# Graph attention with layer norm: the turned source one-hots of two chunks are stored interleaved, element beside element

## The reference, cut to what matters

```python
q = (X @ Wq)[src]; k = (X @ Wk)[dst]
e = tanh(q + k)                               # E x 64
scores = e @ Wphi; scores -= max(scores)
w = exp(scores)
denom = segment_sum(w, src, N)
alpha = w / (denom[src] + 1e-9)
msg = alpha[:, None] * ((X @ Wy_w + Wy_b)[dst] + e @ We)
out = layernorm(X + segment_sum(msg, src, N))
```

## Time and profile before

| | us |
|---|---|
| median of 3 runs | 5431.57 (5428.85 to 5432.63) |
| profiled execution, its own time | 5425.74 |
| span of the profiled execution | 5424.0 |
| busy: PE / DVE / ACT / POOL | 3511.2 / 4216.0 / 3684.6 / 3537.4 |
| indirect gathers of line 1112 | 3276, from 1161.8 to 5309.8 |
| one-hot makers of line 1182 | 206, from 1187.1 to 5291.0 |

### The profile page before, as it was taken

The page is one execution under the profiler, slowest core; times in us unless marked ns, Lnnn a source line. Parts: engine busy times, 40 slices in busy tenths (PEclk is TensorE's granted clock), DMA queues, the critical chain, the costliest instruction groups (busy, mean ns, idle before and its releaser), DMA issues. The chain is left out here.

```text
span 5424.0 us, 91419 instructions
## 1 busy us (share of the span) xinstructions
PE 3511.2 (65%) x19333; PEld 2746.3 (51%) x19333; DVE 4216.0 (78%) x9852; ACT 3684.6 (68%) x14197; POOL 3537.4 (65%) x3559
## 2 busy tenths in 40 slices
PE   7799999955555665555655555556655555556557
PEld 7566566644444444444444444444544444444446
DVE  7699999977777777777777777777777777777776
ACT  3699999966666666666666666666666666666667
POOL 1034434357777777777777777777777777777771
PEclk9899999977777767777777777776677777777778
DMA  3200000023333333333333333333333333333334
GB/s 89 73 5 5 5 5 5 5 71 106 106 106 102 106 106 107 103 106 106 106 103 107 106 105 103 106 107 105 104 106 107 106 103 106 106 105 102 106 98 110
DMA packets 284190, 478.09 MB, mean 88 GB/s; under 512 B 94226, under 2 KB 203892, under 8 KB 283385
## 3 DMA queue, kind: packets, MB, share of 16 engines
q0 software_dynamic: 165184, 324.30, 23.0%
q1 hardware_dynamic: 100662, 142.95, 7.8%
q10 hardware_dynamic: 17794, 4.91, 0.4%
HBM read 456.43 MB, written 20.60 MB: 88 GB/s over the span
## 5 line engine op out<-in xcount | busy, mean ns | idle before, releaser
L1112 POOL DMA_INDIRECT gathered<-table,dst_rows x3276 | 3151.2, 962 | 1008.9 <-issue 992.1
L1146 PE MATMUL bank<-gathered,weighted_onehots 128*128 128x193 f32 x6592 | 1913.4, 455 | 1458.6 <-DVE block_sums L1235 1450.4
L1146 PEld LDWEIGHTS bank<-gathered,weighted_onehots 128*128 128x128 f32 x6592 | 1582.1, 267 | 1661.9 <-issue 997.4
L1235 DVE TENSOR_TENSOR block_sums<-block_sums,bank 128x193 f32 x3296 | 1166.8, 354 | 541.1 <-issue 166.0
L1198 DVE TENSOR_REDUCE gathered<-bank 128x128 f32<-128x384 f32 x1648 | 840.5, 552 | 446.0 <-DMA gathered<-table,dst_rows 435.0
L1157 ACT ACTIVATE gathered<-gathered 128x256 f32<-128x256 f32 x824 | 346.5, 421 | 1202.8 <-DVE gathered L1202 1202.8
L1167 ACT ACTIVATE weighted_onehots<-src_distances,score_less_shift 128x128 f32<-128x128 bf16 x3296 | 1052.4, 390 | 26.9
L1175 ACT ACTIVATE src_distances<-row_to,src_in_block 128x128 bf16<-128x128 f32 x3296 | 1039.6, 386 | 0.0
L822 ACT ACTIVATE places_past_far<-bank,stat 128x98 bf16<-128x98 f32 x2727 | 889.2, 1237 | 18.8 <-PE bank L847 18.8
L822 ACT ACTIVATION_READ_ACCUMULATOR places_past_far<-bank,stat 128x1 f32 x2727 | 887.9, 1097 | 0.0
L1135 PE MATMUL bank<-q_parts,src_onehots_T 128*128 x3296 | 614.7, 317 | 272.6 <-DVE gathered L1202 231.2
(11 more groups left out here) (190 smaller groups left out, 2272.5 us busy)
## 6 DMA issues: line engine op xcount, KB each, us to landing
src_in_block_rows<-src_in_block_list SPq DMA_DIRECT2D x206, 512.0 KB
gathered<-table,dst_rows POOLq DMA_INDIRECT x3276
gathered<-table SPq DMA_DIRECT2D x2560, 0.8 KB
table<-in_x SPq DMA_DIRECT2D x4, 1562.5 KB
x_in<-in_x SPq DMA_DIRECT2D x24, 256.0 KB, 2.9
x_again<-in_x SPq DMA_DIRECT2D x48, 128.0 KB, 2.3
out<-out_rows SPq DMA_DIRECT2D x48, 128.0 KB, 1.9
sorted_list<-sorted_groups,unit_destinations POOLq DMA_INDIRECT x248
```

Source lines behind the costliest of these rows:

```text
L1112: e.indirect_dma_start(slot[:, r, j, 0:ROW], None, table, bass.IndirectOffsetOnAxis(ap=gidx[:, t:t + 1].bitcast(u32), axis=0)).then_inc(ga ...
L1146: made = e.matmul(SM[q % 2 * 2 + j // 2][:, o:o + SUMS], ohw[:, q % 3, j, :], slot[:, r, j, A:SLOT], start=True, stop=True)
L1235: e.tensor_tensor(sums[:, bass.ds(b, SUMS)], sums[:, bass.ds(b, SUMS)], SM[q % 2 * 2 + j // 2][:, o:o + SUMS], ALU.add).then_inc(accumulat ...
```

## The change

The buffer `ohT` keeps its size, but its last two dimensions are swapped. Before, the 2048 bf16 columns of one chunk lay behind the 2048 of the other. Now column `i` of the even chunk lies at place `2 i` and column `i` of the odd chunk at `2 i + 1`. VectorE's compare of line 1182 therefore still reads `lob` element after element, but writes every second bf16 element, and the weight loads in front of the matmuls of line 1135 read every second one. No instruction, wait or transfer is added, removed or moved: the order of the instructions of every engine is the same.

```diff
-        ohT = sb(lists, "src_onehots_T", [PARTS, 2, CHUNK * PARTS], bf16)
+        ohT = sb(lists, "src_onehots_T", [PARTS, CHUNK * PARTS, 2], bf16)
...
-                        made = e.matmul(QK[q % 2][j // 2][:, j % 2 * 3 * A:(j % 2 + 1) * 3 * A], ohT[:, c % 2, o:o + PARTS], q3[:, bass.ds(b, 3 * A)],
+                        made = e.matmul(QK[q % 2][j // 2][:, j % 2 * 3 * A:(j % 2 + 1) * 3 * A], ohT[:, o:o + PARTS, c % 2], q3[:, bass.ds(b, 3 * A)],
                                         start=True, stop=True)
...
-            e.tensor_scalar(ohT[:, c % 2, :], lob[:, c % LOB, :], part0[:, :], None, ALU.is_equal).then_inc(onehots_T_made, 1)
+            e.tensor_scalar(ohT[:, :, c % 2], lob[:, c % LOB, :], part0[:, :], None, ALU.is_equal).then_inc(onehots_T_made, 1)
```

## The result

The changed kernel takes 5556.75 us (median of four, 5554.93 to 5558.66), the kernel before 5430.73 us. The ratio is 1.0228, with a 95% interval from 1.0212 to 1.0243: 126 us slower, where 109 (5540 against 5431.6) were forecast.

What follows compares the result with a forecast made beforehand. The prediction took GpSimd's gathers, held up by VectorE's compare, as the bound. It added 108 us to the profiled 5425.7, giving 5534, or 5540 as a median, 2.0% slower, with a range of 5500 to 5575 us.

Steps and rivals of the forecast that it cites:

- The gathers are the bound and have no slack: GpSimd's gathers, line 1112, run through the main part without a stop, 4148 us from first to last start.
- The compare drops to two elements at a time: Line 1182, writing every second element, falls to 0.517 ns an element from 0.261.
- The rival of the plain rate: Line 1182 falls to one element at a time, 2.33 us, and no longer holds gathers; 5407 us, chance 0.10.
- The length of the compare, 1274 ns: Line 1182: 2048 x 0.517 + 215 = 1274 ns, 0.52 us more than now.
- the hold: While line 1182 runs, VectorE locks GpSimd out of a shared port pair, delaying gathers; 25 us in all before the change.
- the dense middle rate: VectorE's two elements at a time, 0.517 ns an element, taken from four-byte operands in lines 584 and 287.
- The near row, line 589: Nearest profile row with a strided 2-byte output: 242 ns for 124 elements, against 229 at 0.517 ns an element.
- Each hold moves the gather's end by as much as it grows: At line 1112, a compare longer by 0.52 us puts each following gather 0.52 us later; 206 x 0.52 = 108 us.
- The phases stay: Compares keep their places against the gathers; other phases would give 89 to 142 us.
- VectorE's own path costs nothing: 107 us more VectorE busy time, 0.52 of 5.1 us idle in a chunk, is hidden; without cover up to 107 us.
- TensorE's reads cost nothing: Line 1135's weight loads, reading every second element, taken as nothing; at most 0.65 us in a step.

Runs made afterwards that it cites:

- the f32 and strided-source probes: The changed kernel with twelve forms of the compare, six times each, run at its end while other engines are idle; 6183.82 us on another chip.
- the summing form: The compare also sums its output into an unused number, in the changed kernel and in the kernel before; ratios 0.9985 and 1.0010 on another chip.
- the reduction: The kernel before, with an unused VectorE reduction of 1024 numbers added behind each of the 206 compares; 5421.22 us, ratio 0.9987.
- the read-only kernel: The kernel before with its dense compare, but query matmuls read a small fixed buffer of zeros with a step of two; 5426.84 us, ratio 1.0000.
- the kernel with two compares: The kernel before, with the dense compare made twice in a row, the second behind a wait for the first; 5462.36 us, ratio 1.0065.
- write_only: The changed kernel with its strided compare, but query matmuls read a small fixed buffer of zeros without a step; 5557.64 us, ratio 1.0228.
- the kernel with halves: The kernel before, with its dense compare split into two halves, one in this step and one in the next; ratios 1.0012 and 1.0011 on two other chips.

## Why the prediction was right, point by point

- *The gathers are the bound and have no slack.* Right. 128 us more in the gathers are the 126 of the median, and 249 us of other VectorE work changed nothing. It held for the chip of the prediction; on the two others GpSimd also waited for what the profile calls remote, and for TensorE.
- *The compare drops to two elements at a time.* Right, by the f32 and strided-source probes, which take the same time. The rival of the plain rate is out for this compare: it would have taken 2.3 us. Its second half, that a compare at the plain rate does not hold the gathers, is what the summing form showed. As a rule for all lines at the plain rate, which is how I put it, it is wrong: lines 1202 and 1211 delay gathers too (see the end).
- *The length of the compare, 1274 ns.* This is the term that was mis-sized. It measured 1381, so the hold grew by 0.63 us, not 0.52. Of the 107 ns, 85 are the strided output's own, 12 the dense middle rate above my fit, and some 10 the surroundings. The near row, line 589, had said it: 242 ns were 13 above the middle rate, and I set that aside. Put on its 124 elements it is 0.1 ns each, more than the 0.04 that it turned out to be for 2048, but of the right sign. With 0.63 the sum is 206 x 0.63 = 130 us, and 5431.6 + 130 = 5562, 5 us above the median measured.
- *Each hold moves the gather's end by as much as it grows.* Right. Over the 206 compares of the changed kernel (the first at 1191.7 us, the last at 5422.6) the gathers lose 0.76 us in the mean, where 0.12 + 0.63 = 0.75 would follow. By where the compare starts they lose 0.75 us (up to 0.45 behind the gather's start), 0.69 (up to 0.71) and 0.92 (later), in each class 0.6 to 0.65 more than before.
- *The phases stay.* Right: of the 206 compares 159 start within 0.45 us behind a gather's start, of the 206 before 157 did.
- *VectorE's own path costs nothing, TensorE's reads cost nothing.* Both right: the reduction and the read-only kernel.

## What to carry to other kernels

Look for the engine that never waits before the one that is busiest: here GpSimd at 65% set the time, because a gather's 0.95 us and the 0.30 between two leave no gap. When such an engine is GpSimd with indirect DMAs, ask of every VectorE instruction on SBUF not only how long it is but in which form it runs and whether it reads two tensors there. A compare in a fast form that gets slower by a changed step held the gathers longer, while one in the summing form, 2.5 us long, was harmless, and two short holds with a gap are far cheaper than one long one. Swapping the last two dimensions of a buffer is no mere matter of layout if VectorE writes it: here it cost 0.63 us on one instruction in a chunk, and 2.3% in all.

## What the runs showed of the hardware that was not expected

- The compare is not the only thing in the main part that delays gathers. In the timeline of the kernel before, the first line of VectorE below adds two f32 tensors in SBUF, 256 elements in 0.42 us; less the 165 ns that the prediction takes as the fixed part that is 1.0 ns an element, the plain rate. The gather starts under it and ends 0.83 us after it, just as behind a compare:

```profile
1358.08 0.42 DVE L1202 TENSOR_TENSOR gathered<-gathered 128x256 f32<-128x256 f32 x1
1358.17 1.16 POOL L1112 DMA_INDIRECT gathered<-table,dst_rows  x1 [0.30 <-issue]
1358.42 0.42 DVE L1211 TENSOR_TENSOR e_times_phi<-gathered,phi 128x256 f32<-128x256 f32 x1
```

In the main part of the kernel before, every gather that exceeds the median by more than 0.03 us either meets a compare or starts under line 1202 or 1211, whose inputs both lie in SBUF; these cost 22.9 us. Of the 1783 that meet no compare and start under the reductions 1198 and 1213 or under line 1235, which has one input in PSUM, none is delayed. Unlike a compare, lines 1202 and 1211 delay no gather that started before them by holding its end; they are shorter, too. In the kernel with the reduction the gathers at these two lines lose 10.8 us in place of 22.9 and those at a compare 30.1 in place of 25.7, which is the 7.5 us by which its gathers take less time.

- A gap of some 0.04 us between two holds was enough for a gather to end, not to begin and end. In the kernel with two compares the gather had started before the first one, needed only to end, and did so through the gap. Ahead of the main part lines 963 and 965 have such a gap too, but there the gather had started under line 963; by these times it could only begin in the gap, and its end had to wait for line 965. That a gather has two such points, one close behind its start (two gathers of write_only that start 0.05 and 0.06 us ahead of a compare are past it, for they end 0.12 us behind the compare) and one some 0.12 us ahead of its end, is inferred from these ends; no run looked into a gather. That lines 1202 and 1211 delay only the beginning fits it.
- A step of four bf16 elements in the output costs 2495 ns for 2048 (line 1444), 1.8 times the step of two, and as much as the summing form with a step of two, 2480 ns (line 1456). The Trainium skill (SBUF — State Buffer, section Door 1: The DMA port swizzle) has steps of up to 8 bf16 elements free of cost. For a step of two in the source this agrees (1286 ns, as with dense f32); in VectorE's output steps of two and four are not free, and the measurement decides. Whether the step of four still runs in a fast form, and would hold gathers for its 2.5 us, no run shows.
- A scalar read for each partition makes the compare 65 ns longer than a constant does (1371 against 1306, lines 1436 and 1452).
- On the chip where the kernel before took 6091.05 us, the changed kernel with the twelve forms at its end took 6183.82. The forms begin with the row below and fill the last 107 us of the span of 6182.0; two memsets for them start at 6069.1. Without all that about 6071 are left. So in that one run the change cost nothing that shows, although its compare took the same 1.38 us and its gathers lost 150.8 us to it. There the holds take the place of time that GpSimd stands still: from 1200 to 5900 us it waited 552 us for remote and 44 for TensorE, in the kernel with halves on the same chip, whose gathers lose 12.0 us, 632 and 116. How much a hold costs depends on the bound of the chip at hand. Why those two chips were slower stays open.

The tile probe_dense of that kernel (duration ns min/median/max, starts of the first and last):

```profile
L1434 DVE TENSOR_SCALAR probe_dense<-probe_source,probe_source_f x6: 753/753/754, 6074.8 to 6163.8; 128x2048 bf16<-128x2048 bf16 x6
```
